# A fused language-model layer on one core: the opening rearranged, the second item's expansion in idle PSUM banks, gathers first, tail without fillers

## The reference, cut to what matters

```python
h = emb_table[ids]; dom = domain_map[ids]
h = h + sum_d 0.1 * ((h @ W_exp[d].T) @ W_proj[d].T) * (dom == d)      # 8 domains, 32 wide
n = layernorm(h); q, k, v = split(n @ Wqkv.T + b)                      # 16 heads of 16
state_t = retention * state_(t-1) + Gamma * outer(v_t, k_t / 4)        # 16 x 16 per head
y_t = (W_static + state_t) @ q_t
h = h + y @ out_w.T + out_b
n = layernorm(h); xq = round(n / s_x), s_x = max|n| / 127 per token    # weights the same per row
h = h + (xq @ wq.T) * s_x * s_w + bias
```

## Time and profile before

| what | us |
|---|---|
| median of 3 runs (lowest, highest) | 257.43 (255.31, 257.43) |
| the profiled execution's own time | 258.98 |
| its span | 257.1 |
| PE busy | 227.3 (88%) |
| DVE busy | 198.4 (77%) |
| POOL busy | 186.8 (73%) |
| ACT busy | 108.0 (42%) |

### The profile page before, as it was taken

How to read it: one execution, slowest core, us unless ns; L and a number is a source line. 1 busy time by engine, 2 the same in 40 slices (tenths; PEclk the granted TensorE clock), 3 DMA queues, 4 the chain that set the end, 5 groups by cost and what they waited for, 6 DMA issues and landing times.

```text
span 257.1 us, 7827 instructions
## 1 busy us (share of the span) xinstructions
PE 227.3 (88%) x3266; PEld 168.3 (65%) x3266; DVE 198.4 (77%) x391; ACT 108.0 (42%) x272; POOL 186.8 (73%) x97
## 2 busy tenths in 40 slices
PE   5998886998889999999989999998987965868993
PEld 5978644775558586776757767676554853547992
DVE  1027975688966896899799977887899989895773
ACT  6303674135522222697831056977102367100230
POOL 5870009999989999998599995776999999400031
PEclk9999999999999999999999999999999996899998
DMA  5492027411053921101640620025406100110002
GB/s 154 133 273 101 0 84 205 164 45 43 3 146 87 258 88 45 43 1 43 187 145 3 179 70 3 1 72 160 143 3 201 49 4 1 43 41 3 0 3 82
DMA packets 19443, 21.26 MB, mean 83 GB/s; under 512 B 2416, under 2 KB 13904, under 8 KB 19408
## 3 DMA queue, kind: packets, MB, share of 16 engines
q1 hardware_dynamic: 18640, 18.65, 23.3%
q0 software_dynamic: 768, 2.11, 3.4%
HBM read 14.98 MB, written 5.77 MB: 81 GB/s over the span
## 4 chain that ended last, share of the span: by engine, by line
PE 69%; DVE 13%; issue 6%; ACT 4%; DMA 3%; POOL 2%; another core or an unknown queue 1%; SPq 0%; DVEq 0%; ACTq 0%; POOLq 0%
PE y_ps L1127 10%; PE scr L978 10%; PE w_ps L1110 8%; PE scr L955 6%; PE q_ps L1072 5%; PE scr L992 5%; PE scr L1007 4%; PE scr L968 4%; PE scr L932 3%; PE y_ps L1072 3%; DVE zz L896 3%; PE scr L1031 3%; PE scr L1045 3%; POOL uu L447 2%; PE y_ps L1121 2%
## 5 line engine op out<-in xcount | busy, mean ns | idle before, releaser
L447 POOL TENSOR_TENSOR uu<-vg,kk 128x1024 f32<-128x1024 f32 x64 | 150.8, 2392 | 32.0 <-DMA vg<-v_far 19.3
L896 DVE TENSOR_TENSOR zz<-e_hg,q_ps 128x1524 f32<-128x1524 f32 x32 | 55.3, 1728 | 0.0
L867 DVE TENSOR_TENSOR_SCAN e_hg<-decay,w_ps 128x512 f32<-128x512 f32 x32 | 39.0, 1218 | 10.3 <-PE w_ps L1110 9.8
L1110 PE MATMUL w_ps<-uu,comb 128*32 128x128 f32 x1024 | 35.3, 277 | 1.5 <-POOL uu L447 1.1
L1110 PEld LDWEIGHTS w_ps<-uu,comb 128*32 128x32 f32 x1024 | 27.5, 111 | 9.0 <-issue 7.9
L1127 PEld LDWEIGHTS y_ps<-zz,coll 128*32 128x32 f32 x768 | 19.8, 111 | 19.4 <-issue 8.7
L1127 PE MATMUL y_ps<-zz,coll 128*32 128x128 f32 x768 | 28.2, 281 | 4.7 <-DVE zz L896 4.7
L406 POOL TENSOR_TENSOR tok_dom<-tok_dom,bf 128x1024 f32<-128x1024 f32 x4 | 8.7, 2186 | 21.0 <-DVE tmp_b L710 21.0
L527 ACT ACTIVATE junk<-tok_dom 128x256 bf16<-128x256 f32 x24 | 9.7, 407 | 28.6 <-DVE tok_dom L664 28.6
L882 DVE TENSOR_TENSOR zz<-e_hg,q_ps 128x512 f32<-128x512 f32 x32 | 21.7, 679 | 0.0
L396 POOL DMA_INDIRECT tok_dom<-in_table,ids_sb x16 | 15.5, 969 | 6.2 <-issue 3.5
(11 more groups left out here) (124 smaller groups left out, 390.5 us busy)
## 6 DMA issues: line engine op xcount, KB each, us to landing
vg<-v_far SPq DMA_DIRECT2D x32, 256.0 KB, 4.2
v_far<-v_sb SPq DMA_DIRECT2D x8, 256.0 KB, 4.0
out_h<-tok_dom SPq DMA_DIRECT2D x8, 256.0 KB, 2.1
k_far<-kk SPq DMA_DIRECT2D x12, 128.0 KB
k_sb<-k_far SPq DMA_DIRECT2D x4, 384.0 KB, 3.2
wexp<-in_w_exp SPq DMA_DIRECT2D x1, 256.0 KB
tok_dom<-in_table,ids_sb POOLq DMA_INDIRECT x16, 5.0
wproj<-in_w_proj SPq DMA_DIRECT2D x1, 256.0 KB
```

Source lines behind the costliest of these rows:

```text
L447: pool.tensor_tensor(uu[:, g % NU, two], v_of.to_broadcast(shape), k_of.to_broadcast(shape), ALU.mult).then_inc(s_u, 1)
L867: dve.tensor_tensor_scan(states(g).rearrange("p a m -> p (a m)"), decay[:, NA * n:NA * (n + 1)].rearrange("p a m -> p (a m)"), w.rearrange ...
L896: dve.tensor_tensor(z, e.to_broadcast(shape), q.to_broadcast(shape), ALU.mult).then_inc(s_z, 1)
L1110: last = pe.matmul(w_ps[32 * hp:32 * hp + 32, g % NW, a], comb[:, NA * n + a, hp], uu[:, g % NU, hp, a], start=True, stop=True, skip_group ...
```

## The change

- Item 0's statistics: both halves are added and measured, then one square root and one rstd1 serve all four tiles (`tiles` no longer halves them for the first layer norm). ScalarE normalises half 0 (xhat 0.0); VectorE normalises half 1 in a new stage `first` and also evacuates its transposes (a new VectorE stage `xhat_t`). A new semaphore, `s_first`, stands for VectorE's half.
- Item 1's expand goes to the two banks of `w_ps` and its dom to a bank of `q_ps`, with semaphores of their own. base_t 1.0, base_t 1.1, dom 1.0 and expand 1.0 stand behind corr 0.1, expand 1.1 between q 0.0 and v 0.1. On VectorE, w_comb comes first, then mask 1.0 and 1.1, and then w_amax and the rest. The first two combines wait for the masks.
- All sixteen gathers stand in slot -1; the second item's come ahead of decays. `after` has no entry any more.
- On SP, copy_k 0.0 and copy_v 0.1 have moved: copy_k 0.0 ahead of group 1's v rows, copy_v 0.1 ahead of group 2's.
- The tail has 24 filler matmuls behind attn 3.1 instead of 36, and none behind xq_t 3.0 (4 and 5 before) and ffn 3.1 (3 before). Fillers of the opening fall from 31 to 5 beside the 18 ahead of it.
- Many entries of the loop stand a slot or two elsewhere. GpSimd's bias of item 3 waits for both of VectorE's last steps (`s_last` 2).

```diff
 PE_CALENDAR = """
-    -1: base_t 0.0, base_t 0.1, wake 0.4, dom 0.0, expand 0.0, expand 0.1, corr 0.0, corr 0.1, wake 0.16, xhat_t 0.0,
-    wake 0.8, xhat_t 0.1, wake 0.3, v 0.0, k 0.0, q 0.0, v 0.1, k 0.1, base_t 1.0, q 0.1; 0: dom 1.0; 2: base_t 1.1,
-    expand 1.0, expand 1.1; 4: w_t 0.0; 5: pair0 0.0; 6: corr 1.0, pair1 0.0; 8: corr 1.1; 10: w_t 0.1; 11: fix 0.0;
...
-    wake 3.8; 138: attn_pre 3.0; 139: attn 3.0, attn_pre 3.1, attn 3.1, wake 3.36, xq_t 3.0, wake 3.4, wake 3.5, ffn
-    3.0, xq_t 3.1, ffn 3.1, wake 3.3
+    -1: base_t 0.0, base_t 0.1, wake 0.3, dom 0.0, expand 0.0, expand 0.1, corr 0.0, corr 0.1, base_t 1.0, base_t 1.1,
+    dom 1.0, expand 1.0, xhat_t 0.1, xhat_t 0.0, wake 0.2, v 0.0, k 0.0, q 0.0, expand 1.1, v 0.1, k 0.1, q 0.1; 5:
+    pair0 0.0, w_t 0.0; 6: pair1 0.0; 7: corr 1.0; 9: corr 1.1; 10: w_t 0.1; 11: w_row 0.0; 12: fix 0.0; 16: xhat_t
+    1.0, xhat_t 1.1; 17: v 1.0; 18: k 1.0; 20: k 1.1; 24: v 1.1, pair1 0.1; 26: pair0 0.1; 27: q 1.0; 28: fix 0.1; 31:
...
+    2.0; 121: xq_t 2.1, ffn 2.1; 122: pair0 3.1; 123: pair1 3.1; 127: fix 3.1; 130: wake 3.8; 135: attn_pre 3.0; 138:
+    attn 3.0; 139: attn_pre 3.1, attn 3.1, wake 3.24, xq_t 3.0, ffn 3.0, xq_t 3.1, ffn 3.1
 """
 ACT_CALENDAR = """
-    -1: sigmoid 0.0, base_t 0.0, domain 0.0, base_t 0.1, dom 0.0, w_scale 0.0, sqrt1 0.0, xhat 0.0, sqrt1 0.1, xhat_t
-    0.0, xhat 0.1, xhat_t 0.1, bo_hi 0.0, w_round 0.0, v 0.0, bo_mid 0.0, b_scale 0.0, k 0.0, bo_lo 0.0, q 0.0, v 0.1,
-    k 0.1, q 0.1; 3: base_t 1.0, domain 1.0; 4: dom 1.0; 5: base_t 1.1, w_t 0.0; 6: moments1 1.0; 7: w_t 0.1; 8:
...
+    -1: sigmoid 0.0, base_t 0.0, domain 0.0, base_t 0.1, dom 0.0, w_scale 0.0, domain 1.0, base_t 1.0, base_t 1.1,
+    sqrt1 0.1, xhat 0.0, xhat_t 0.0, dom 1.0, bo_hi 0.0, b_scale 0.0, v 0.0, k 0.0, q 0.0, w_round 0.0, v 0.1, bo_mid
+    0.0, k 0.1, bo_lo 0.0, q 0.1; 4: w_t 0.0; 6: moments1 1.0, w_t 0.1; 7: moments1 1.1; 8: sqrt1 1.1; 9: w_row 0.0;
+    10: xhat 1.0, xhat 1.1; 12: xhat_t 1.0, xhat_t 1.1; 15: v 1.0, k 1.0; 19: k 1.1; 25: v 1.1, y 0.0; 28: q 1.0; 30:
...
 DVE_CALENDAR = """
-    -1: w_ret 0.0, mask 0.0, mask 0.1, stat1 0.0, rstd1 0.0, stat1 0.1, rstd1 0.1, w_amax 0.0, w_comb 0.0, bo_less
-    0.0, bo_less2 0.0, w_int 0.0, w_coll 0.0, w_lag 0.0; 1: mask 1.0, qk 0.0; 2: mask 1.1, gv0 0.0; 4: stat1 1.0; 6:
-    gv1 0.0; 8: stat1 1.1; 9: rstd1 1.1; 12: qk 0.1; 26: gv0 0.1; 27: gv1 0.1; 31: qk 1.0; 33: mask 2.0; 35: mask 2.1,
...
+    -1: w_ret 0.0, mask 0.0, mask 0.1, stat1 0.0, stat1 0.1, rstd1 0.1, first 0.1, xhat_t 0.1, w_comb 0.0, mask 1.0,
+    mask 1.1, w_amax 0.0, bo_less 0.0, bo_less2 0.0, w_int 0.0, w_coll 0.0, w_lag 0.0; 1: qk 0.0; 2: gv0 0.0; 5: stat1
+    1.0, gv1 0.0; 8: stat1 1.1; 11: rstd1 1.1; 13: qk 0.1; 26: gv0 0.1; 27: gv1 0.1; 31: qk 1.0; 34: mask 2.0; 35:
...
 SP_CALENDAR = """
-    -1: copy_v 0.0; 1: copy_v 0.1; 3: copy_k 0.0; 4: read_k 0.0; 8: copy_v 1.0; 9: copy_k 1.0; 10: copy_v 1.1, read_k
-    1.0; 16: copy_v 2.0; 19: copy_k 2.0, read_k 2.0; 20: copy_v 2.1, store 0.0; 21: store 0.1; 24: copy_v 3.0; 27:
-    copy_k 3.0, read_k 3.0; 28: copy_v 3.1, store 1.0; 29: store 1.1; 32: store 2.0, store 2.1, store 3.0, store 3.1
+    -1: copy_v 0.0; 1: copy_k 0.0; 2: copy_v 0.1; 3: read_k 0.0; 7: copy_v 1.0; 9: copy_k 1.0; 11: copy_v 1.1; 12:
+    read_k 1.0; 15: copy_v 2.0; 20: copy_k 2.0, copy_v 2.1, read_k 2.0, store 0.0, store 0.1; 23: copy_v 3.0; 28:
+    copy_k 3.0, copy_v 3.1, read_k 3.0, store 1.0, store 1.1; 32: store 2.0, store 2.1, store 3.0, store 3.1
 """
 POOL_CALENDAR = """
-    -1: gathers 0.1, gathers 0.0, decays 0.0, gathers 2.0, gathers 1.1, gathers 1.0; 18: after 0.1; 24: gathers 2.1;
-    26: gathers 3.0; 30: gathers 3.1; 67: bias 0.0; 74: out 0.0, out 0.1; 99: bias 1.0; 106: out 1.0, out 1.1; 127:
-    bias 2.0, out 2.0, out 2.1, bias 3.0, out 3.0
+    -1: gathers 0.1, gathers 0.0, gathers 1.0, gathers 1.1, decays 0.0, gathers 2.0, gathers 2.1, gathers 3.0, gathers
+    3.1; 71: bias 0.0; 72: out 0.0, out 0.1; 103: bias 1.0; 104: out 1.0, out 1.1; 127: bias 2.0, out 2.0, out 2.1,
+    bias 3.0, out 3.0
 """
 
@@ -134,8 +133,10 @@
     SLOTS = range(-1, (NC + 1) * UNITS)
 
     uses = [("attn", c, h) if name == "attn_pre" else (name, c, h) for slot in SLOTS
-            for name, c, h in pe_at.get(slot, []) if name not in ("wake", "fix") and (name, c) != ("attn", NC - 1)]
+            for name, c, h in pe_at.get(slot, []) if name not in ("wake", "fix") and (name, c) not in (("attn", NC - 1), ("expand", 1), ("dom", 1))]
     use = {key: (n % 2, n // 2) for n, key in enumerate(uses)}
+    use.update({("expand", 1, h): (2 + h, 0) for h in range(2)})
+    use["dom", 1, 0] = 4, 0
 
     def group(g):
 
@@ -245,6 +246,8 @@
         am = r_ps[:, 104:108]
 
         scr_two = [scr[:, i, :].rearrange("p (b d) -> p b d", b=2) for i in range(2)]
+        scr_two += [w_ps[:, i].rearrange("p (b a) m -> p b (a m)", b=2) for i in range(NW)]
+        row_of = {0: scr[:, 0, :], 1: scr[:, 1, :], 4: q_ps[:, 0, :]}
         scr_bf = [scr[:, i, 0:T // 2].bitcast(BF16).rearrange("p (k t) -> p k t", k=KD) for i in range(2)]
 
         s_ids = sem("s_ids")
@@ -262,8 +265,8 @@
         s_coll = sem("s_coll")
         s_lagw = sem("s_lagw")
         s_sig = sem("s_sig")
-        s_full = [sem("s_full0"), sem("s_full1")]
-        s_free = [sem("s_free0"), sem("s_free1")]
+        s_full = [sem("s_full0"), sem("s_full1"), sem("s_full_w0"), sem("s_full_w1"), sem("s_full_q")]
+        s_free = [sem("s_free0"), sem("s_free1"), sem("s_free_w0"), sem("s_free_w1"), sem("s_free_q")]
         s_mean = [sem("s_mean1"), sem("s_mean2")]
         s_var = [sem("s_var1"), sem("s_var2")]
         s_sqrt = [sem("s_sqrt1"), sem("s_sqrt2")]
@@ -280,6 +283,7 @@
         s_round = sem("s_round")
         s_xq = sem("s_xq")
         s_last = sem("s_last")
+        s_first = sem("s_first")
         s_h2b = sem("s_h2b")
         s_out = sem("s_out")
         s_stored = sem("s_stored")
@@ -304,7 +308,7 @@
 
         def tiles(n, c, h):
 
-            if on_vector(n, c):
+            if (n, c) == (1, NC - 1):
                 return slice(2 * h, 2 * h + 2), 1
             return slice(0, TT), 2
 
@@ -399,7 +403,7 @@
 
                 pool.wait_ge(s_xhat[1], 2 * c + (2 if c < NC - 1 else 1))
                 if c == NC - 1:
-                    pool.wait_ge(s_last, 1)
+                    pool.wait_ge(s_last, 2)
                 if c == 0:
                     pool.wait_ge(s_w_back, 80)
                 h = tok[:, TT * c:TT * c + TT, :]
@@ -617,7 +621,7 @@
                 if c >= 1:
                     taken(act, "expand", c - 1, 0)
                     taken(act, "expand", c - 1, 1)
-                act.activation(dom_row[:], scr[:, bank, :], ACT.Copy).then_inc(s_free[bank], 1)
+                act.activation(dom_row[:], row_of[bank], ACT.Copy).then_inc(s_free[bank], 1)
 
             stage = {"base_t": evacuate("base_t", emb_t, ("expand", None)), "domain": domain, "dom": dom,
                      "xhat_t": evacuate("xhat_t", act_t, ("q", 1)), "q": q, "v": v, "k": k, "y": y, "moments1": moments(0, "corr"),
@@ -710,6 +714,19 @@
                     last = dve.tensor_scalar(tmp_b[:, t, :], tok[:, TT * c + t, :], rstd[:, 1, t:t + 1],
                                              nmr[:, 1, t:t + 1], ALU.mult, ALU.add)
                 last.then_inc(s_last, 1)
+
+            def first(c, h):
+
+                dve.wait_ge(s_rstd[0], 2)
+                for t in (2 * h, 2 * h + 1):
+                    last = dve.tensor_scalar(tmp_f[:, t, :], tok[:, TT * c + t, :], rstd[:, 0, t:t + 1],
+                                             nmr[:, 0, t:t + 1], ALU.mult, ALU.add)
+                last.then_inc(s_first, 1)
+
+            def xhat_t(c, h):
+
+                bank = filled(dve, "xhat_t", c, h)
+                dve.tensor_copy(act_t[:, :, T // 2 * h:T // 2 * (h + 1)], scr_two[bank]).then_inc(s_free[bank], 1)
 
             def whole(c, h):
 
@@ -899,7 +916,7 @@
             stage = {"mask": mask, "stat1": stats(0, "corr"), "rstd1": rsqrt(0), "stat2": stats(1, "attn"),
                      "rstd2": rsqrt(1), "amax": amax, "scaled": scaled, "w_amax": w_amax, "bo_less": bo_less,
                      "bo_less2": bo_less2, "w_int": w_int, "w_ret": w_ret, "w_comb": w_comb, "w_coll": w_coll,
-                     "w_lag": w_lag, "normal": normal, "whole": whole, "last_out": last_out, "qk": qk, "gv0": gv(0), "gv1": gv(1)}
+                     "w_lag": w_lag, "normal": normal, "first": first, "xhat_t": xhat_t, "whole": whole, "last_out": last_out, "qk": qk, "gv0": gv(0), "gv1": gv(1)}
             for slot in SLOTS:
                 g, a = divmod(slot, NA)
                 if 0 <= g < NC * GROUPS:
@@ -941,7 +958,7 @@
                 if c == 0:
                     pe.wait_ge(s_cast, 1)
                 for t in range(TT):
-                    last = pe.matmul(scr[:, bank, P * t:P * t + P], dom_b[:, TT * c + t:TT * c + t + 1]
```

(7 more changed lines are left out.)

49 lines of the change are left out of this document (23 added, 26 removed).

## The result

| | us |
|---|---|
| before, median (lowest to highest) | 256.8 (255.31 to 257.43), 4 runs |
| after, median (lowest to highest) | 264.44 (262.7 to 266.79), 4 runs |
| ratio, with its 95% interval | 1.0284 (1.0192 to 1.0375) |
| profiled execution of after, its span | 263.51, 261.7 |

By the medians the change makes the kernel 7.6 us slower; by the ratio it is 1.9 to 3.8% slower.

A forecast was written before the change was run, and what follows sets the result against it. TensorE was taken to bound the full middle, so only the opening, head and tail could change the time: 3.4 later at the head (opening's 1.1 included), 1.9 back in the tail, +1.5 on 257.43, giving 258.9; 8-in-10 range 254.3 to 261.8.

The forecast's parts named there:

- the last line of the sum: Whole kernel: the shown runs' median, 257.43, lies 1.55 below the profiled execution; adding 1.5 gives 258.9.
- The opening gains 1.1.: Opening, up to GpSimd's first product: one square root instead of two saves 1.38, base_t 1.1 ahead of it loses 0.25.
- rival 1: Opening: the signal at 20.09 is not late in the new kernel, everything behind moves by 1.7, 257.2; chance 0.20.
- So I let bo_less2 wait for the second product's end: Loop's head: VectorE's preparations start at 42.9, end at 48.5 and release the third product; combine 1 is 3.4 later.
- rival 3: Loop's head: GpSimd's first product keeps out w_amax's second step, combine 1 is 4.9 late, 260.4; chance 0.20.
- SP's order, my main argument: Loop's head: group 1's v rows, now behind copy_k, are issued at 43.0 instead of 38.90 and land at 46.9.
- Everything from combine 1 to combine 2 and on keeps its spacing.: Loop after combine 1: the head's 3.4 delay is carried unchanged into the full middle.
- rival 4: Opening: its removed fillers were needed, TensorE's clock falls, 5.8 us twice, above 263; chance 0.05.
- I count nothing for them: Loop: six gathers leave it, 6 to 7 in all, but TensorE decides from group 2 on, so 0.
- The changed order of the middle: 0, with 1 us either way.: Middle of the loop: the changed order leaves the same work on TensorE, so 0, 1 us either way.
- The tail, 1.9.: Behind the last projection: with fewer fillers and a later GpSimd bias, VectorE's last addition starts 1.9 earlier.
- Rival 2: Loop's head: the v rows come in time, combine 1 is 2.2 early, with the tail 253.3; chance 0.13.

The follow-up runs named there:

- b_gf_tail: Kernel before with all gathers first, 24 tail fillers in place of 48, and GpSimd's last bias behind both VectorE steps: 258.04, ratio 1.0055.
- a_amax_early: Changed kernel with w_amax ahead of w_comb on VectorE, SP's new order kept: 260.87, ratio 1.0178.
- after_again: Changed kernel, nothing altered, run again on another chip: 264.96, ratio 1.0282 to the kernel before.
- a_filled: Changed kernel with 36 fillers on TensorE between combine 0 and combine 1: 262.79, ratio 1.0283.
- b_gathers_first: Kernel before with all sixteen gathers in the opening, the second item's ahead of decays: 253.53, ratio 0.993.
- b_fewer_fillers: Kernel before with 24 tail fillers in place of 48, GpSimd's bias left as before: 255.36, ratio 0.9942.
- the h kernels: Three hybrids: kernel before with the tail's edits and item 0 normalised in one go, gathers as before, two fewer early, or all first: ratios 0.9971, 1.0033, 1.0138.
- a_gathers_late: Changed kernel with the gathers of items 2 and 3 put back into the loop: 262.66, ratio 1.0322.
- b_tail: Kernel before with 24 tail fillers in place of 48 and GpSimd's last bias behind both VectorE steps: 254.91, ratio 0.9895.
- b_tail_again: Kernel before with 24 tail fillers and the later GpSimd bias, run once more with more rounds: 255.58, ratio 0.9947.
- a_sp_order: Changed kernel with SP's first entries as in the kernel before: 254.07, ratio 0.9987.
- b_held_again: Kernel before with the second item's gathers and those behind them held until corr 0.1 is over, second run: 257.61, ratio 1.0052.
- h_two_fewer: Kernel before with the tail's edits, item 0 normalised in one go, and item 2's first-half gathers moved into the loop: 258.18, ratio 1.0033.
- the first group: Four runs on one chip: gathers first or held in the kernel before; later gathers or SP's old order in the changed one: ratios 0.993, 0.9999, 1.0322, 0.9987.

## Why the prediction was wrong, step by step

The profiled execution came to 263.51 where the sum had 260.5: 3.0 of the miss of 5.5 is in the steps, what is left of 8.2 of loss and 5.2 of gain that the sum lacked. The other 2.5 is in the last line of the sum, "the runs shown had a median of 257.43, 1.55 below the profiled one": I carried that over, but the changed kernel's median lies 0.9 above its profiled execution. The steps:

1. **"The opening gains 1.1."** It lost 3.4: off by 4.5, the largest error. The late signal at 20.09 was seen and named, but taken as a fixed thing (or, in rival 1, as something that may go away). It was not asked what makes it and whether the change moves it. The gathers ran beside it in the trace of before; the change prolongs them to 26.2, and puts base_t 1.x, whose signals are late too, ahead of the square root on ScalarE. "This cover must hold" was said of those gathers' landing, which was fine; their side effect was the price. The counting of the root was right where no signal is late: the changed opening is 0.8 to 1.7 shorter there (24.6 and 25.2 against 26.0 and 26.3). What the sum also lacked is the clock behind the late base_t: the expansion took 1.7 more. The fillers taken out are not to blame for that, as b_gf_tail, which keeps them, lost more there (6.48 instead of 3.67).
2. **"So I let bo_less2 wait for the second product's end", combine 1 25.6 behind v 0.0.** It was 27.2: off by 1.6. The last wait was another one than in the forecast. VectorE's chain ended at 52.8 and held nothing; the third product waited for its rows until 54.80. They were late by k 0.1 (evacuated 15.9 behind v 0.0 where the sum has 13.8) and by a landing of 5.07, outside the bound of 4.3. k 0.1 was that late by rival 3, which had this stretch at 27.1 with w_amax's step kept out. It "decides if the product starts before w_amax's second step"; the product began at 40.99, the step at 41.40. a_amax_early puts a price on it: 3.9. SP's order, my main argument, is 2.0 to 2.5, and nothing once w_amax is early.
3. **"Everything from combine 1 to combine 2 and on keeps its spacing."** It grew by 2.1, and by 4.3 in after_again. I wrote that TensorE "only idles in its place" and did not ask what an idle TensorE does to its clock; rival 4 asked it of the opening alone. a_filled has 5.2 in this column at the full clock, so the clock is most of that term.
4. **"I count nothing for them" (the gathers in the loop), "because GpSimd only gets further ahead".** The column to group 8 is 3.1 shorter. b_gathers_first has 2.0 of it in the old order. The rest is no gain of the gathers: a_filled, where combine 2 is nearly on time, takes 33.2 there and b_gathers_first 33.1, so some 1.1 is what the kernel catches up behind a late combine 2. "From group 2 on" had no row behind it: the earlier trace rows are from the full middle, and the gathers of the loop ran from 69.70 to 83.9, before group 8 (89.7).
5. **"The changed order of the middle: 0, with 1 us either way."** 2.1 faster from group 8 to 31. The order gives about 1, and the rest goes with the clock near the loop's end (same columns as in the earlier trace rows, before, then after):

```profile
214.00:221.00 7.00, 5.96 (x70) 3.84 (x74) 5.68 (x14) 3.16 (x6) 5.56 (x4) 0.52 0.00 1
223.00:227.00 4.00, 3.52 (x52) 2.45 (x56) 3.90 (x10) 2.75 (x5) 4.00 (x2) 0.57 0.02 6
```

   The kernels with the old order and the long stretch of lower clock have 136.1 to 136.8 in this column (b_fewer_fillers, with one stretch more, aside), those with the old order and the short one (b_gathers_first, the h kernels) 135.3 to 135.5, the changed order with the short one 133.5 to 134.6 (a_gathers_late, with its waits, aside). No run changed that clock by itself.
6. **The tail, 1.9.** Measured 1.8 in every kernel that has both edits. The split between the two edits was needless: with fewer fillers GpSimd's bias is worth nothing, whichever way it waits.

So the errors were +4.5, +1.6, +2.1 and -5.2 (steps 4 and 5), which make the 3.0. The forecast's sign was right, but that the miss is no larger is luck: two sums of errors, 8.2 and 5.2, cancel in part. Rival 1 came half true: the addition follows corr 0.0 at once, at 21.98, and other signals are late in its place. Rival 2 is out. Rival 3 named the right mechanism for the head, with an opening 4.5 too early; its end at 260.4 missed by 4.0, the same errors in the other steps and the 2.5 of the medians. Rival 4's sign, a half-speed slice in the opening, did show (0.50 from 15 to 18), but not its price: v, k and q of half 0 took 1.98, 1.95 and 1.98; only q 0.1 was slow (3.65 at 45.52), and nothing on the path to combine 1 stood behind it. That the time is above 263, as rival 4 has it, is chance.

An estimate from the table shows where the loss of the traces lies. Without late signals v 0.0 starts near 26.0 in the old opening (25.9 and 26.2 in b_tail and b_tail_again, whose opening is that of before) and at 25.2 in the changed one (a_sp_order), 2.9 and 7.2 earlier than in the traces compared here. Taken off the last additions (253.8 and 258.4) that leaves 250.9 and 251.2, next to no difference. So by this estimate the loop and the tail about pay for the head, and what makes the changed kernel slower is that late signals cost it more. This was not measured: both traces of the full change have them.

The Trainium skill ("SBUF — State Buffer", Who interferes with whom) says that a tensor_scalar can take the port pair that VectorE shares with GpSimd, and that the order of issue decides who waits, for the whole length of the other's instruction. The traces agree: line 773, a tensor_scalar on two numbers per partition, takes 1.96 behind a product and 0.17 without one.

## What to carry to other kernels

Before moving work into an idle place, list what the idle time held up and what it covered: here it kept TensorE's clock up and let VectorE prepare between GpSimd's products. Cut both traces at the same few starts and compare differences; a median that mixes two edits misled me by a factor of four. Read the granted clock in each piece too: a pause of TensorE anywhere can slow what follows it. A wait that the profile puts down to "remote" deserves the question of what runs beside it, ahead of any sum that moves that neighbour.

## What the hardware showed that I had not expected

- TensorE's signals can arrive 1 to 4 us late while GpSimd issues indirect gathers: the transposes of base_t 1.1, over at 25.11, are seen at 27.84 after, 1.7 behind the end of the last gather (26.18). A wait "remote" of ScalarE or VectorE stands in the opening of 12 of the 20 traces. Where no gather ran when the correction ended (b_held_again, h_two_fewer, on chips where other traces have late signals), its signal was not late; with one it is not always late (b_tail's addition starts at 17.1), and in the four traces of the first group it never was. Two traces make the gathers likely as the cause; they don't show it. What delays the signal inside the chip stays open, and so does why it comes and goes.
- A step on 128x2 numbers can cost nearly a whole outer product (1.96 of 2.37), and five small ones in a row, each meeting a product, took 12 for 1.8.
- Behind an idle stretch of 7 to 11 us between combine 0 and combine 1 TensorE's granted clock is at the lower level: the columns from combine 1 to 2 are 6.6, 6.7, 6.7, 6.7, 8.9 and 9.0 in the six kernels with it, against 4.6. What decides between 6.7 and 8.9 was not tried.
